# First hats by halves of four tiles, a far count inside the offset convolution, VectorE's loop turned at a box sum, and small products moved down

## What is computed

```python
# layer 0: 3 offset/mask channels from a 3x3 conv; one bilinear sample per point; depthwise 3x3, pointwise 1x1
off = conv3x3(xn, w_off) + b_off                  # 3 channels
samp = grid_sample_bilinear(xn, grid + off[0:2]) * sigmoid(off[2])
x = x + pointwise(depthwise3x3(samp))
# layer 1: average pool, then a modulated deformable 3x3 convolution
p = avg_pool3(xn)
dy, dx = conv3x3(p, off_w)                        # 18 channels
mask = 2 * sigmoid(conv3x3(p, mod_w))             # 9 channels
x = x + deform_conv2d(p, dy, dx, mask, w) + b     # 9 taps, each a bilinear sample
# layer 2: 3x3 convolution whose weights are made once from weight, its sign and r_matrix
x = x + conv3x3(xn, w2) + b2
# layer 3: two strip attentions with 5 taps each (horizontal, vertical), a channel gate, pointwise out
x = x + proj_out(...)
```

## Time and profile before

| what | us |
|---|---|
| median of 3 runs | 1719.94 |
| lowest, highest | 1717.85, 1722.87 |
| the profiled execution | 1719.42 |
| its span, first to last instruction | 1717.6 |
| TensorE busy in the span | 1591.8 |
| VectorE, ScalarE, GpSimd busy | 1141.4, 659.3, 50.2 |
| mean granted TensorE clock | 0.958 of 2.4 GHz |

### The profile page before, as it was taken

The page is one execution under the profiler, slowest core; times in us unless marked ns, Lnnn a source line. Parts: engine busy times, 40 slices in busy tenths (PEclk is TensorE's granted clock), DMA queues, the critical chain, the costliest instruction groups (busy, mean ns, idle before and its releaser), DMA issues.

```text
span 1717.6 us, 22494 instructions
## 1 busy us (share of the span) xinstructions
PE 1591.8 (93%) x7252; PEld 837.6 (49%) x7252; DVE 1141.4 (66%) x2139; ACT 659.3 (38%) x1066; POOL 50.2 (3%) x76
## 2 busy tenths in 40 slices
PE   2979999999999999999999999999999999999975
PEld 1537453565435554365534645355543655337422
DVE  4358349864598457883498835985469844887266
ACT  2126224461345413453244622555134541346131
POOL 2000000000000000000000000000000000000000
PEclk8989999999999999999999999999999999999987
DMA  3000000100001000000001000010000100000000
GB/s 117 14 13 2 7 1 1 51 5 4 1 1 52 7 2 1 26 27 7 1 1 51 2 6 1 1 52 7 2 1 14 39 7 2 1 25 2 1 0 25
DMA packets 7971, 24.61 MB, mean 14 GB/s; under 512 B 1664, under 2 KB 2368, under 8 KB 7792
## 3 DMA queue, kind: packets, MB, share of 16 engines
q1 hardware_dynamic: 7792, 22.40, 3.5%
HBM read 12.13 MB, written 8.39 MB: 12 GB/s over the span
## 4 chain that ended last, share of the span: by engine, by line
PE 75%; DVE 11%; issue 6%; ACT 4%; SPq 3%; DMA 1%; POOL 1%; DVEq 0%; POOLq 0%; ACTq 0%
PE psN L516 14%; PE psO L516 13%; PE psN L851 11%; PE psO L720 7%; PE psN L720 5%; PE psN L627 4%; PE psO L576 4%; SPq L414 3%; ACT samp L932 2%; DVE samp L1662 2%; PE psN L594 2%; PE psN L558 2%; PE psN L564 2%; PE psM L500 2%; PE psN L901 1%
## 5 line engine op out<-in xcount | busy, mean ns | idle before, releaser
L516 PE MATMUL psO<-samp,w 128*128 128x512 f32 x576 | 285.2, 631 | 0.0
L516 PE MATMUL psN<-xn,w 128*128 128x512 f32 x576 | 278.7, 605 | 1.7 <-DVE yout L1409 0.9
L1143 ACT ACTIVATE samp<-psN,vec 128x512 f32<-128x512 f32 x160 | 110.0, 687 | 130.4 <-PE psN L851 130.4
L516 PEld LDWEIGHTS psO<-samp,w 128*128 128x128 f32 x576 | 106.6, 200 | 102.6 <-issue 96.2
L1317 DVE COPY xblk<-psN 120x256 f32<-120x256 f32 x128 | 54.3, 424 | 142.7 <-PE psN L558 142.7
L932 ACT ACTIVATE samp<-psN 128x576 f32<-128x576 f32 x192 | 118.2, 676 | 58.1 <-PE psN L627 58.0
L516 PEld LDWEIGHTS psN<-xn,w 128*128 128x128 f32 x576 | 98.3, 189 | 84.5 <-issue 84.5
L932 ACT ACTIVATE G<-psN 120x256 f32<-120x256 f32 x128 | 49.1, 383 | 229.6 <-PE psN L564 229.6
L720 PE MATMUL psN<-img,w 128*128 128x512 f32 x288 | 133.4, 608 | 0.0
L720 PE MATMUL psO<-img,w 128*128 128x512 f32 x288 | 133.0, 603 | 0.0
L627 PE MATMUL psN<-GQt,xq 64*128 64x144 f32 x1536 | 123.1, 297 | 10.6 <-ACT samp L932 9.0
(11 more groups left out here) (156 smaller groups left out, 2299.9 us busy)
## 6 DMA issues: line engine op xcount, KB each, us to landing
xin<-in_x SPq DMA_DIRECT2D x16, 512.0 KB, 4.1
out<-yout SPq DMA_DIRECT2D x16, 512.0 KB, 3.7
pool_v<-rows SPq DMA_DIRECT2D x72, 25.5 KB
w<-in_w SPq DMA_DIRECT2D x2, 576.0 KB, 5.1
samp<-in_r SPq DMA_DIRECT2D x1, 576.0 KB, 6.8
tab<-in_tab SPq DMA_DIRECT2D x1, 513.0 KB, 5.3
kh_w<-in_kh SPq DMA_DIRECT2D x1, 320.0 KB, 5.4
kv_w<-in_kv SPq DMA_DIRECT2D x1, 320.0 KB, 5.6
```

The source lines that it names most:

```text
L516: last = mm(dst[:, h, :], wgt[:, k, :], rhs(h, k), start=(k == 0), stop=(k == K9 - 1))
L1143: nc.scalar.activation(out, bank(m)[0:out.shape[0]], fn, **kw).then_inc(l3_act.sem, 1)
```

## The change

Six things are changed together.

- `hats(s, b)` makes the hats of four tiles, b = 0 or 1; `hf` is laid out by halves, and so is the mask `mk`. For image 0 VectorE makes the first half, loads the flag, branches, and makes the second half between the transposition of the fourth tile and the product of the fifth. For image 1 both halves come ahead of the flag.
- `offset_parts` signals after each half of the image, `parts` copies and signals each half, and `offsets` takes the tiles in the order 0, 2, 4, 6, 1, 3, 5, 7, waiting for the first half ahead of tile 0 and for the second ahead of tile 1.
- `far(i, 2)` stands between the two halves of `offset_parts(3)`.
- VectorE's box sum of image 1 moves from the end of the pass to the head of the next (and of the last pass), so that `store_ready(1)` comes ahead of it.
- `next_offsets` moves from hook (1, 3) to (1, 6), `start_far` from (1, 6) to (1, 8).
- The seven `start_hat` steps come behind the statistics of L2B and ahead of its affine terms.

```diff
-DVE_STEPS = 142
+DVE_STEPS = 156
...
-START_STEPS = 43
+START_STEPS = 40
...
-        hy4 = [hf[s][:, 0:TEK * QR].rearrange("p (t e k a) -> p t e k a", e=PAIRS, k=K9, a=QR) for s in range(2)]
-        hx8 = [hf[s][:, TEK * QR:].rearrange("p (t e k b) -> p t e k b", e=PAIRS, k=K9, b=QB) for s in range(2)]
+        TK = TEK // 2
+        hf_half = [hf[0][:, TK * (QR + QB) * b:TK * (QR + QB) * (b + 1)] for b in range(2)]
+        hy4 = [t[:, 0:TK * QR].rearrange("p (t e k a) -> p t e k a", e=PAIRS, k=K9, a=QR) for t in hf_half]
+        hx8 = [t[:, TK * QR:].rearrange("p (t e k b) -> p t e k b", e=PAIRS, k=K9, b=QB) for t in hf_half]
...
                         last = mm(dst[32 * g:32 * g + 32, h, :], w[:, k, :], window(src)(h, k),
                                   start=(k < 4), stop=(k >= K9 - 4), skip_group_check=True)
-                last.then_inc(parts_product.sem, 1)
+                    last.then_inc(parts_product.sem, 1)
+                    if h == 0:
+                        between()
...
-                pe.wait_ge(parts_ready.sem, parts_ready.at(i, max(n, 1)))
...
-                for t in range(TILES):
+                for t in (0, 2, 4, 6, 1, 3, 5, 7):
+                    if t < 2:
+
+                        pe.wait_ge(parts_ready.sem, parts_ready.at(i, (1, 2 * n - 2 + t)[n > 0]))
...
-                offset_parts(3, img[1], w1off)
-                far(i, 2)
+                offset_parts(3, img[1], w1off, lambda: far(i, 2))
...
                             hooks[0, 3] = next_rows
-                            hooks[1, 3] = next_offsets
-                            hooks[1, 6] = lambda: start_far(i + 1)
+                            hooks[1, 6] = next_offsets
+                            hooks[1, 8] = lambda: start_far(i + 1)
...
-                act.wait_ge(parts_product.sem, parts_product.at(i, n - 1))
                 for b in range(2):
-                    last = copy(off_parts[s].rearrange("p (j b r c) -> p j b r c", b=2, j=STRIPS, c=SW)[:, :, b],
-                                psO[s][:, b, :].rearrange("p (r j c) -> p j r c", j=STRIPS, c=SW))
-                last.then_inc(parts_ready.sem, 1)
+                    act.wait_ge(parts_product.sem, parts_product.at(i, 2 * n - 3 + b))
+                    copy(off_parts[s].rearrange("p (j b r c) -> p j b r c", b=2, j=STRIPS, c=SW)[:, :, b],
+                         psO[s][:, b, :].rearrange("p (r j c) -> p j r c", j=STRIPS, c=SW)).then_inc(parts_ready.sem, 1)
...
-                def hats(s):
+                def hats(s, b):
...
-                    own.step(v_.scalar_tensor_tensor(hf[s][:], hf[s][:], -1.0, hf[s][:], ALU.mult, ALU.max))
+                    half = hf_half[b]
+                    own.step(v_.scalar_tensor_tensor(half, half, -1.0, half, ALU.mult, ALU.max))
...
+                for part in range(4):
+                    pool3(own, 1, part, i, FIRST)
                 for s in range(2):
                     dve.wait_ge(offs_ready.sem, offs_ready.at(i, 2 + s))
...
-                    hats(s)
+                    hats(s, 0)
+                    if s:
+                        hats(s, 1)
...
                     with dve.If(far > 0):
+                        if s == 0:
+                            hats(s, 1)
...
+                        for n in range(TILES):
+                            if s == 0 and n == STRIPS:
+                                turn(n - 1)
+                                hats(s, 1)
+                                hat_product(n)
+                                continue
+                            hat_product(n)
                             if n:
...
+                                turn(n - 1)
+                        turn(TILES - 1)
...
                         start_flag(own, i + 1)
-                        for part in range(START_HAT):
-                            start_hat(own, i + 1, 0, part)
...
                     stats(own, ("L2A", "L2B")[s], order)
+                    if s and more:
+                        for part in range(START_HAT):
+                            start_hat(own, i + 1, 0, part)
                     affine(own, ("L2A", "L2B")[s], order)
...
                     affine_scale(own, "L1B", order)
-                    for part in range(4):
-                        pool3(own, 1, part, i, order)
                 store_ready(1)
...
-                for part in range(4):
+                for part in range(0 if s else 4):
                     pool3(first, s, part, 0, FIRST)
```

More of the change, by code:

```diff
@@ L260, in conv_preact_kernel @@
         strip8_ready = signal("strip8_ready", 2)
[L261 removed]
+        parts_product = signal("parts_product", 4)
         rows_product = signal("rows_product", 1)
         rows_ready = signal("rows_ready", 1)
[L264 removed]
+        parts_ready = signal("parts_ready", 5)
         xT_product = signal("xT_product", 2)
@@ L479, in group_mean, with offset_parts @@
                 mm(ps[SAMPLE[name]][:, 0:2], gavg, g[:, 12:14], start=True, stop=True).then_inc(group_ready.sem, 1)
-            def offset_parts(n, src, w):
+            def offset_parts(n, src, w, between=lambda: None):
                 dst = psO[n % 2]
@@ L1495, in next_affine @@
                         affine(own, ("S0", "S1")[k], order)
[L1497 removed]
+                def hats(s, b):
                     for e in range(PAIRS):
[L1500 to L1501 removed]
+                        shift = om2[:, e].rearrange("p g (j b k) -> p g b j k", b=2, k=K9)
+                        for axis, h, at_e, m in ((0, hy4[b], T_EY, QR), (1, hx8[b], T_EX, QB)):
                             own.step(v_.tensor_tensor(
                                 h[:, :, e], tab[:, at_e:at_e + K9 * m].rearrange("p (k b) -> p k b", b=m).unsqueeze(1)
[L1504 to L1505 removed]
+                                .broadcast_to((C, STRIPS, K9, m)),
+                                shift[:, axis, b].unsqueeze(3).broadcast_to((C, STRIPS, K9, m)), ALU.subtract))
                     own.settle()
[L1507 removed]
+                    half = hf_half[b]
+                    own.step(v_.scalar_tensor_tensor(half, half, -1.0, half, ALU.mult, ALU.max))
                     own.settle()
[L1509 removed]
+                    own.step(v_.tensor_scalar(half, half, 1.0, 1.0, ALU.min, ALU.subtract))
                     own.settle()
                     dve.wait_ge(mask_ready.sem, mask_ready.at(i, 3 + s))
[L1513 to L1515 removed]
+                    flat = half[:, TK * QR:].rearrange("p (e b) -> p e b", b=QB)
+                    own.step(v_.scalar_tensor_tensor(flat, flat, 2.0, mk[s][:, TK * b:TK * (b + 1)].unsqueeze(2)
+                                                     .broadcast_to((C, TK, QB)), ALU.mult, ALU.mult))
                     own.settle()
@@ L1578, in one_pass @@
                     with dve.Else():
[L1579 to L1590, removed]
-                            if n:
[L1592 to L1598, removed]
-                                    .then_inc(q_G.sem, 1)
@@ new lines, in one_pass, with hat_product @@
+                        hy, hx = ([h.rearrange("p t e k b -> p t (e k) b") for h in both] for both in (hy4, hx8))
+                        def hat_product(n):
+                            o = TILES * s + n
+                            if o >= 2:
+                                dve.wait_ge(q_G.sem, q_G.at(i, o - 1))
+                            b, j = n // STRIPS, n % STRIPS
+                            v_.tensor_tensor(GQ[n % 2][:].rearrange("p (k a b) -> p k a b", a=QR, b=QB),
+                                             hy[b][:, j].unsqueeze(3).broadcast_to((C, PAIRS * K9, QR, QB)),
+                                             hx[b][:, j].unsqueeze(2).broadcast_to((C, PAIRS * K9, QR, QB)),
+                                             ALU.mult).then_inc(q_GT.sem, 1)
@@ new lines, in turn @@
+                        def turn(n):
+                            o = TILES * s + n
+                            dve.wait_ge(q_GT.sem, q_GT.at(i, o + 1))
+                            if o >= RING:
+                                dve.wait_ge(q_smp.sem, q_smp.at(i, PAIRS * (o - RING + 1)))
+                            v_.transpose(GQt[o % RING][:].rearrange("p e k r c -> p (e k r c)"), GQ[n % 2][:])\
+                                .then_inc(q_G.sem, 1)
+                        for n in range(TILES):
[5 more added lines that the diff above has]
+                            hat_product(n)
+                            if n:
+                                turn(n - 1)
```

4 lines of the change are left out of this document (2 added, 2 removed).

## The result

The changed kernel takes 1689.85 us (median of 4 runs, 1687.2 to 1690.4) against 1719.64 for the kernel before, measured beside it; the ratio is 0.9822 with a 95% interval of 0.9804 to 0.984. The forecast was 1690.9. The number was right and half of the reasons were not: place A gave 7.5 us more than forecast and place B, where I had put a gain of 1.6, lost 4.7. The experiments took the two apart.

A forecast was written before the change was run, and what follows sets the result against it. TensorE, busy for 93% of the span, was taken to set the time, with gains where it stands still or runs slowly. Gains of 26.9 us at place A and 1.6 at place B took 28.5 from 1719.4: 1690.9 us, range 1683 to 1702.

The forecast's parts named there:

- place A: Last convolution of the second layer, where TensorE waits for the copied gather before narrow products; gain 26.9 us.
- place B: Head of a pass, from offset convolution through first sampling; only VectorE's chain counts; gain 0.2 us a pass, 1.6 in all.
- The wait at place A: Narrow products three taps later find their data with 0.7 us to spare; 13.4 us gained in seven passes.
- The clock at place A: Half clock behind the wait cost 18.7 us; 17.5 counted as regained, less 4.0 for narrow products still lowering it.
- Rival 1: Narrow products at place A bring the clock down by themselves, once in each pass; 1698.8 us, chance 0.15.
- Offset parts in halves, and the turned loop: At place B the copies' wait of 1.19 us goes, om starts that much earlier; the turn costs nothing.
- Rival 4: At place B the halves don't take the copies' wait away; 9.5 us lost, 1700.4 us, chance 0.03.
- rival 3: VectorE's loop turn is exposed ahead of the box sum; free to 0.8 us, decides from 4.4; chance 0.03.
- Hats in halves: Seven more instructions for each image lengthen VectorE's chain at place B by 1.05 us, bounds 0.56 and 1.05.
- The flag's count: Moved inside the offset convolution it costs its 0.25 us wherever it stands; VectorE asks later, so nothing.
- The clock at B: Doubling om at low clock costs 0.54 us a pass; half of it taken away, +0.27.
- The new wait ahead of the fifth tile: TensorE waits 1 to 2.6 us in the first sampling; clock loss between 0 and 3.4 us, taken as 0.2.

The follow-up runs named there:

- e2: The changed kernel with place A put back as in the kernel before; 1724.5 us, ratio 1.0044.
- e3: The changed kernel with the hats in one piece for each image, as before; 1683.8 us, ratio 0.9798.
- e4: The changed kernel with VectorE's loop turned behind the box sum of the second image, where it was before; 1686.7 us, ratio 0.982.
- e5: The changed kernel with both output stores cut to 64 of 1024 points for each channel; 1684.6 us, ratio 0.9804.
- e9: e4 with VectorE's loop turned in its longest idle stretch, ahead of start_offsets at place A; 1680.6 us, ratio 0.9777.
- e6: e1 with the offsets of layer 0 at tap (1, 4) instead of (1, 6), leaving about half the wait; 1699.7 us, ratio 0.989.
- e1: The kernel before with the change at place A alone; 1681.7 us, ratio 0.9786.

## Why the prediction was right, and where it was not

*What bounds the kernel.* Right: both places were where the difference lies, and at place B only VectorE's chain counts. In all kernels here the first sampling ended 2.25 to 2.28 us behind the last transposition, but for passes in which the clock fell in the sampling.

*The wait at place A.* Right in mechanism and size: 13.4 us gone, data there before TensorE, the statistics done 1.0 us and the first hat product started 1.2 us ahead of TensorE, where I had said 0.8 and one.

*The clock at place A.* The mechanism right, the term mis-sized. I left 4.0 us of loss for narrow products that bring the clock down by themselves, and they brought it down in no pass; and I counted 17.5 of the 18.7 us, since narrow products would hardly be slowed. They were: the 54-row products took 20.3 us in all before and 17.2 after. Of the 7 x 4.9 = 34.4 us of the place, 32.2 lie between the end of the second sampling and the start of the next convolution (the ten products at 789.25). 13.4 of these are the wait, and the other 18.8 are just what the granted clock accounts for: before, it was low for 6.8 us in four passes and for 3.4 in three, 37.5 us at half speed. So the clock gave 18.8 where I had put 13.5. The last 2.2 us, 0.3 a pass, stand in the 22 products of that convolution, which took 9.9 to 10.5 us before and 9.9 after, at full clock in both kernels; their cause stays open. Rival 1 did not come about.

*Offset parts in halves, and the turned loop.* This is the step that failed. I wrote that the wait of 1.19 us goes "and om starts that much earlier", with the turn costed at nothing since it "lies between 726.79 and 727.57, at most 0.78". The gap bounded only the part of the turn that showed. What the runs show is that the turn takes 3.0 to 4.5 us from the start of the last instruction before it in five kernels (the changed one, e2, e3, e4 and e5), 1.8 us or more of it idle, that stores don't change it, and that om moves forward by 1.7 us where the turn alone is put elsewhere. In the kernel before, only 1.9 to 2.3 us lie between the start of the output addition and om, but 3.1 to 3.5 between the start of the last box addition and om, against 3.0 in e4. So it looks as if the turn began beside the output addition there.

The transfers of the kind "instruction" in the traces (`q14 instruction` on the page) bear this out. In each turn one of 8 KB stands there. In the kernel before, it starts 0.03 to 0.06 us behind the start of the output addition, while VectorE is busy with it. In e4 it starts 1.1 us behind the start of the last box addition in five turns, and 2.2 behind it in the sixth, which is the turn of 4.1 us instead of 3.0. In both kernels om starts 1.5 to 1.6 us behind its landing (1.8 once, where the narrow products ended later). In the changed kernel two such transfers stand in each turn, and the box sum starts 0.9 to 1.7 us behind the landing of the last. Whose instructions they carry isn't recorded; and behind the loop the kernel before has one of them with no idle time (om 0.4 us behind it), so a transfer alone is not the wait. What the turn spends its time on is therefore argued, not shown.

Of the 1.19 us a pass that I counted, 0.2 came in the mean, and it came in the two passes that have no turn of the loop before them: 1.2 us in the last (om at 6.9) and 0.9 in the first, whose start lies 0.4 us later. In the six others om came 0.07 us later in the mean than before. Rival 4 did not come about: the wait of 1.19 us went in every pass. So rival 3 came about, in its mechanism: I had given it 0.8 us of room and it stood open for some 2.2 (1.9 to 2.7). With the price per us that I gave, 1.4 us in six passes, it takes back 8.4 us. It didn't reach the point of decision, 4.4 us. The Trainium skill, "Runtime: NRT & Kernel Launch", section "Instruction fetch mechanics", says that a taken branch out of the fetched pages stalls on a fetch; the idle time of 1.9 to 2.7 us agrees with it, and I had let a gap of the profile overrule the rule without asking what stood in front of the gap.

*Hats in halves.* The mechanism right, the size too large: +1.05 us on the chain forecast, 0.67 measured, between the bounds of 0.56 and 1.05. The 1.1 us between the changed kernel and e3 would seem to confirm the forecast, but 0.28 of them are clock in the doubling and 0.18 the wait for the flag. That the early tiles give nothing was right.

*The flag's count.* I costed it at nothing, as VectorE asks later. In the two passes with the long fall of the clock at place B it came too late, since TensorE's half convolution before it took longer: VectorE waited 1.1 us for it in all, 0.14 a pass. The line says so: `PE psM L640: 1.1, 2`.

*The clock at B.* I took half of the loss in the doubling away. With the longer wait for om the clock still fell in seven of the eight passes; the doubling takes 1.44 us in the mean against 1.54. The new wait ahead of the fifth tile, which I put at 0.2 us, cost nothing in seven passes, because TensorE came late to the sampling; in the first pass 0.8. It showed its price when om came early (e9). The last transposition ended 31.1 us behind the start of the pass in the mean, where I had wanted to see 30.

Sum at B, a pass: forecast 1.19 - 1.05 + 0.27 - 0.2 = 0.2; measured 0.21 - 0.67 + 0.10 - 0.10, and 0.14 for the flag, = -0.6. Together: forecast 26.9 at A and 1.6 at B; measured 34.4 and -4.7. The errors are of opposite sign, and the forecast of 28.5 met 29.6 by that, which is luck.

## What to carry to other kernels

A gap shows only the part of a loop's turn that stands open: cost the turn from where it can have begun, beside the instructions ahead of it, and put it where the engine waits anyway. A wait of one us on TensorE can cost more than itself if narrow products stand next to it; removing the wait gave back more in clock (18.8 us) than in waiting (13.4). Splitting a step to start its consumer sooner gives nothing if the consumer's end hangs on the last piece, and each added instruction costs something on the chain, here 0.10 us. Two runs that differ in one edit can also differ in clock: compare passes with the same clock before a difference is put down to the edit.

## What the runs showed of the hardware

- VectorE's turn of this loop takes 3.0 to 4.5 us from the start of the instruction before it to the start of the one behind it, 1.8 us or more of it idle; 512 KB stores beside it make no difference (3.2 to 4.0 us with them, 3.6 to 4.0 with 32 KB). Set beside a wait of 8.9 us it costs nothing visible.
- The clock stays at 2.4 GHz through 2 us of six-column products with wide ones on both sides (seven passes of seven in the changed kernel). With 1.0 us of standing before them it fell to 1.2 in six of seven (e6), with 1.9 us in seven of seven (before) and six of seven (e2).
- In the first sampling, with products of 144 columns on both sides, it fell behind waits of 2.0 to 2.1 us in six passes of six (e9). Behind waits of 1.5 to 1.8 us it fell in four passes of seven (the changed kernel, e2, e4, e5), and behind those up to 1.3 us in none.
- At place B the same order of work let the clock fall in some passes and not in others: in the first run above it fell in four of the six middle passes (e1), with the wait for the copies 1.2 us long in all, and once behind a wait for om of 0.5 us where it did not fall behind one of 1.0. What decides there was not settled.
